# Output projection of a token-mixing stage: one full-precision product against three products of rounded parts, with GpSimd making one of the parts

## The reference

```
h = attention(x)                       # softmax(q k / 4) v, then the output projection w_out, b_out
h = concat([cls, h], tokens)
u = layernorm(h)
h = h + ssm(u)                         # Bu = u B_w.T; h_t = W h_{t-1} + Bu_t; y = hs C_w.T + D * u
u2 = layernorm(h)
shared = (silu(u2 Wg_s.T) * (u2 Wu_s.T)) Wd_s.T
p = sigmoid(u2 Wr.T + rb); the two best experts of 8 for each token
h = h + shared + sum over chosen e of p_e * expert_e(u2)
```

## Time and profile before

| | us |
|---|---|
| median of 3 runs | 1158.5 (1157.01 to 1158.73) |
| time of the profiled execution | 1163.81 |
| its span, first to last instruction | 1161.9 |
| around the span | 1.9 |
| PE busy | 1116.7 (96%) |
| DVE busy | 916.8 (79%) |
| ACT busy | 584.2 (50%) |
| POOL busy | 394.3 (34%) |
| mean granted TensorE clock | 0.987 |

### The profile page before, as it was taken

How to read it: one execution, slowest core, us unless ns; L and a number is a source line. 1 busy time by engine, 2 the same in 40 slices (tenths; PEclk the granted TensorE clock), 3 DMA queues, 4 the chain that set the end, 5 groups by cost and what they waited for, 6 DMA issues and landing times.

```text
span 1161.9 us, 22261 instructions
## 1 busy us (share of the span) xinstructions
PE 1116.7 (96%) x6090; PEld 718.5 (62%) x6091; DVE 916.8 (79%) x1571; ACT 584.2 (50%) x973; POOL 394.3 (34%) x508
## 2 busy tenths in 40 slices
PE   9999999999999999989999999969999999999996
PEld 5654333333333333477777787757888888888885
DVE  4788888888888887678888888777777777777774
ACT  4445777777777777631233222432444444444442
POOL 2002621011111101214345443353555555554553
PEclk9998999999999999989999999999999999999998
DMA  7887333332333322041244541122333333333332
GB/s 232 273 273 259 92 89 88 93 99 81 95 85 90 103 72 87 1 164 42 68 109 109 100 98 39 38 47 78 55 55 54 51 56 52 51 53 54 54 55 32
DMA packets 109714, 105.37 MB, mean 91 GB/s; under 512 B 42464, under 2 KB 97904, under 8 KB 109648
## 3 DMA queue, kind: packets, MB, share of 16 engines
q1 hardware_dynamic: 92704, 85.38, 26.2%
q0 software_dynamic: 16960, 19.38, 10.5%
HBM read 64.88 MB, written 39.68 MB: 90 GB/s over the span
## 4 chain that ended last, share of the span: by engine, by line
PE 73%; DVE 10%; issue 3%; POOL 3%; ACT 1%; another core or an unknown queue 0%; DMA 0%; POOLq 0%; DVEq 0%; ACTq 0%
PE mix_pairs L73 20%; PE pv L688 11%; PE by_key L675 10%; PE by_query L666 9%; PE mix_made L1874 9%; PE mix_turn L1861 3%; POOL kept_table L1130 3%; PE mix_made L1282 2%; PE mix_made L1270 2%; PE by_query L709 2%; PE mix_turn L1841 1%; PE mix_pairs L1308 1%; PE mix_made L1253 1%; DVE mix_stats L1462 1%; DVE k_mix_u L1472 1%
## 5 line engine op out<-in xcount | busy, mean ns | idle before, releaser
L762 DVE TENSOR_REDUCE k_neg_max<-by_query 128x2 f32<-128x1024 f32 x240 | 282.8, 1220 | 48.4 <-PE by_query L666 45.2
L823 ACT ACTIVATE k_wu_e<-by_key 128x512 f32<-128x512 f32 x512 | 270.1, 600 | 64.9 <-PE by_key L675 64.8
L675 PE MATMUL by_key<-k_wg_e 99*128 99x512 bf16 x512 | 175.1, 384 | 2.8 <-PEq L147 2.4
L1818 POOL DMA_INDIRECT out_rows<-x_y,k_slot x72 | 114.0, 1583 | 156.1 <-PE mix_turn L1841 104.6
L666 PE MATMUL by_query<-k_wg_e 96*128 96x512 bf16 x480 | 144.7, 382 | 0.0
L1918 ACT ACTIVATE x_gate<-mix_pairs 128x512 f32<-128x512 f32 x72 | 43.0, 597 | 196.8 <-PE mix_pairs L73 196.8
L688 PE MATMUL pv<-k_wu_e,k_wd_e 128*17 128x512 f32 x1024 | 134.5, 598 | 0.3 <-ACT k_wu_e L823 0.3
L73 PE MATMUL mix_pairs<-w_short,x_T 128*128 x288 | 120.8, 419 | 2.2 <-issue 2.2
L1874 PEld LDWEIGHTS mix_made<-x_wd,x_acts_T 128*128 128x128 f32 x864 | 111.2, 188 | 7.4 <-ACT x_acts_T L1941 0.9
L73 PE MATMUL mix_pairs<-w_short,x_rest 128*128 x288 | 113.9, 396 | 0.0
L1874 PE MATMUL mix_made<-x_wd,x_acts_T 128*128 128x256 f32 x864 | 112.6, 279 | 0.7 <-ACT x_acts_T L1941 0.7
(11 more groups left out here) (251 smaller groups left out, 1960.8 us busy)
## 6 DMA issues: line engine op xcount, KB each, us to landing
k_wg_e<-kept_qk SPq DMA_DIRECT2D x384, 64.0 KB, 2.3
kept_qk<-k_qk_parts SPq DMA_DIRECT2D x32, 384.0 KB, 3.4
kept_v<-k_v_ones SPq DMA_DIRECT2D x8, 544.0 KB, 5.3
k_wd_e<-kept_v SPq DMA_DIRECT2D x32, 136.0 KB, 2.7
k_wu_e<-in_xT SPq DMA_DIRECT2D x8, 512.0 KB, 4.6
kept_heads<-k_wd_e SPq DMA_DIRECT2D x8, 512.0 KB, 3.0
k_heads_in<-kept_heads SPq DMA_DIRECT2D x8, 512.0 KB
k_wg_e<-in_wg_e SPq DMA_DIRECT2D x8, 512.0 KB, 4.7
```

What stands on the lines that cost most here:

```text
L675: pe.matmul(by_key[:, key_bank(job), :], k_rows[0:SROWS, g, h, kt * P:(kt + 1) * P], q_rows[0:SROWS, g, h, :], start=True, stop=True).then ...
L762: dve.tensor_reduce(neg_max[:, g % 2, 2 * n:2 * n + 2], by_query[:, bank:bank + 2, :], AX.X, ALU.max, negate=True).then_inc(query_read, 1)
L823: act.activation(probs[:, key_tile(j) // 2 * G + j // 2 % G, j % 2, :], by_key[:, key_bank(job), :], ACT.Exp, scale=float(HD) ** -0.5).the ...
L1818: pool.indirect_dma_start(out=dram["out"], in_=y[:, r % 2, :], in_offset=None, compute_op=ALU.add, out_offset=bass.IndirectOffsetOnAxis(ap ...
```

## The change

The change has four parts.

1. For images 2 to 7, `project_out` takes three fp32r products (`split_products`) in the place of one float32 product per tile and chunk. It needs the rounded part and the rest of `heads_T` and of `wo_T`. ACT makes the rounded parts `heads_short` (128x1024, once for each of the images 2 to 7, in steps 1 to 6) and `wo_short` (128x512, once, in step 1), right behind its copy of `heads_T`. POOL makes the rests in place, right behind `+ h` and ahead of the power for the second layer norm: `mix_heads_T_rest` occupies the place of `heads_T`, `wo_T_rest` that of `wo_T`. Images 0 and 1 keep the float32 product.
2. `u2` is turned, rounded, cut and copied bank by bank: `u2_turned` is told after each of the two banks, and the three instructions on 128x1024 become three times two on 128x512 in steps 0 to 6. Step 7 keeps whole instructions.
3. The new tiles `heads_short` and `wo_short` lie where `wd_e` of experts 4 and 5 comes to lie, so these two matrices are loaded in step 7, behind the store of image 6's output, and no longer in steps 3 and 4.
4. Several semaphores of the class token are merged into one (`cls_products`), with the same waits in the same order.

The diff, cut to what does this:

```diff
@@ SP
-                for name in ("wg_e", "wu_e", "wd_e") if e < E - 2 else ("wg_e", "wu_e"):
+                for name in ("wg_e", "wu_e", "wd_e") if e < EARLY_DOWN else ("wg_e", "wu_e"):
...
                 if nxt:
                     load_expert(b + 1)
+                elif this:
+                    load_late("out_made", 2 * B, range(EARLY_DOWN, E - 2))
...
-                    load_late()
+                    load_late("gate_made", FC * B, (E - 2, E - 1))
@@ POOL, in step
                     pool.tensor_tensor(rows, rows, h[:, :, :], ALU.add).then_inc(ev["ud_done"], 1)
+                    if b == 1:
+                        pool.wait_ge(ev["heads_shortened"], 1)
+                        pool.wait_ge(ev["out_made"], 2 * (b + 1))
+                        pool.tensor_tensor(short(wo_parts[1][:, :, :]), mem["wo_T"][:, :, :], wo_parts[0][:, :, :],
+                                           ALU.subtract).then_inc(ev["heads_cut"], 1)
+                    if nxt and prev:
+                        pool.wait_ge(ev["heads_shortened"], b + 1)
+                        pool.tensor_tensor(short(heads_rest), heads_T, heads_parts[0][:, :, :],
+                                           ALU.subtract).then_inc(ev["heads_cut"], 1)
                     inverse_deviation(b, 2)
@@ ACT, in step
                 if nxt:
                     copy_turned(heads_T, b + 1, "heads_turned", "hT_copied")
+                if b == 1:
+                    act.activation(short(wo_parts[0][:, :, :]), mem["wo_T"][:, :, :],
+                                   ACT.Copy).then_inc(ev["heads_shortened"], 1)
+                if nxt and prev:
+                    act.wait_ge(ev["hT_copied"], b + 2)
+                    act.activation(short(heads_parts[0][:, :, :]), heads_T, ACT.Copy).then_inc(ev["heads_shortened"], 1)
                 if prev:
                     silu(b - 1, 3)
...
-                    copy_turned(short(u2_short), b, "u2_turned", "shared_shortened")
-
-                    act.wait_ge(ev["u2_cut"], b + 1)
-                    copy_turned(u2_T, b, "u2_turned", "u2T_copied")
+                    for c in range(DC):
+                        act.wait_ge(ev["u2_turned"], DC * b + c + 1)
+                        act.activation(short(u2_short[:, c, :]), turn[:, c, :], ACT.Copy).then_inc(ev["shared_shortened"], 1)
+
+                    for c in range(DC):
+                        act.wait_ge(ev["u2_cut"], DC * b + c + 1)
+                        act.activation(u2_T[:, c, :], turn[:, c, :], ACT.Copy).then_inc(ev["u2T_copied"], 1)
@@ PE
+                        if parts:
+                            mm = split_products(pe, to, [part[:, c, t * P:(t + 1) * P] for part in lhs],
+                                                [part[:, c, :] for part in w], start=(c == 0), stop=(c == DC - 1))
...
-                by_token(heads_T, mem["wo_T"], "out_made", tiles)
+                if b < 2:
+                    by_token(heads_T, mem["wo_T"], "out_made", tiles, False)
+                else:
+                    pe.wait_ge(ev["heads_cut"], b)
+                    by_token(heads_parts, wo_parts, "out_made", tiles, True)
@@ DVE, cut_second
+                    for c in range(DC):
+                        dve.wait_ge(ev["shared_shortened"], 2 + DC * b + c + 1)
+                        dve.tensor_tensor(short(u2_rest[:, c, :]), turn[:, c, :], u2_short[:, c, :],
+                                          ALU.subtract).then_inc(ev["u2_cut"], 1)
```

More of the change, by code:

```diff
@@ L903 @@
 EARLY = 5
+EARLY_DOWN = 4
 def shorten_weights(act, mem, n):
@@ L948, in stage_mix @@
             for n in ("mix_heads_T", "mix_u_T", "mix_hidden", "mix_u2_T", "u2_short", "u2_rest"))
+        heads_rest = mem["mix_heads_T_rest"][:, :, :].rearrange(by_feature, c=DC)
+        heads_parts, wo_parts = (mem["heads_short"], heads_rest), (mem["wo_short"], mem["wo_T_rest"])
         h2 = sb("mix_h2", [P, 2, TT, D], FP32)
@@ L1032, in load_expert, with load_late @@
             def load_expert(e):
-                for name in ("wg_e", "wu_e", "wd_e") if e < E - 2 else ("wg_e", "wu_e"):
+                for name in ("wg_e", "wu_e", "wd_e") if e < EARLY_DOWN else ("wg_e", "wu_e"):
                     sp.dma_start(mem[name][:, bass.ds(e, 1), :, :], dram[name][:, bass.ds(e, 1), :, :]
                                  ).then_inc(mem["expert_in"][e] if e < 3 else mem["experts_in"], 16)
-            def load_late():
-                sp.wait_ge(ev["gate_made"], FC * B)
-                for e in (E - 2, E - 1):
+            def load_late(free, count, which):
+                sp.wait_ge(ev[free], count)
+                for e in which:
                     sp.dma_start(mem["wd_e"][:, bass.ds(e, 1), :, :], dram["wd_e"][:, bass.ds(e, 1), :, :]
@@ L1203, in step @@
                 if last:
-                    copy_turned(u2_T, b, "u2_turned", "u2T_copied")
-                    act.wait_ge(ev["u2T_copied"], b + 1)
-                    act.activation(short(u2_short[:, :, :]), u2_T[:, :, :], ACT.Copy).then_inc(ev["shared_shortened"], 1)
+                    act.wait_ge(ev["u2_turned"], DC * (b + 1))
+                    act.activation(u2_T[:, :, :], turn[:, :, :], ACT.Copy).then_inc(ev["u2T_copied"], DC)
+                    act.wait_ge(ev["u2T_copied"], DC * (b + 1))
+                    act.activation(short(u2_short[:, :, :]), u2_T[:, :, :], ACT.Copy).then_inc(ev["shared_shortened"], DC)
                 elif this:
-                    copy_turned(short(u2_short), b, "u2_turned", "shared_shortened")
-                    act.wait_ge(ev["u2_cut"], b + 1)
-                    copy_turned(u2_T, b, "u2_turned", "u2T_copied")
+                    for c in range(DC):
[4 more added lines that the diff above has]
+                        act.activation(u2_T[:, c, :], turn[:, c, :], ACT.Copy).then_inc(ev["u2T_copied"], 1)
                 if this:
@@ L1233, in _, with turn_rows @@
         def _(pe):
-            def turn_rows(rows, done, to=turn):
+            def turn_rows(rows, done, to=turn, by_bank=False):
                 for c in range(DC):
@@ L1237, in turn_rows @@
                         mm = pe.transpose(to[:, c, t * P:(t + 1) * P], rows[:, t, c * P:(c + 1) * P], ident[:, :])
-                mm.then_inc(ev[done], 1)
+                    if by_bank:
+                        mm.then_inc(ev[done], 1)
+                if not by_bank:
+                    mm.then_inc(ev[done], 1)
             def turn_heads(b):
@@ L1476, in cut_second @@
             def cut_second(b):
-                dve.wait_ge(ev["shared_shortened"], 2 + b + 1)
-                dve.tensor_tensor(short(u2_rest[:, :, :]), turn[:, :, :] if b < B - 1 else u2_T[:, :, :], u2_short[:, :, :],
-                                  ALU.subtract).then_inc(ev["u2_cut"], 1)
+                if b == B - 1:
+                    dve.wait_ge(ev["shared_shortened"], 2 + DC * B)
+                    dve.tensor_tensor(short(u2_rest[:, :, :]), u2_T[:, :, :], u2_short[:, :, :],
+                                      ALU.subtract).then_inc(ev["u2_cut"], DC)
+                else:
+                    for c in range(DC):
+                        dve.wait_ge(ev["shared_shortened"], 2 + DC * b + c + 1)
+                        dve.tensor_tensor(short(u2_rest[:, c, :]), turn[:, c, :], u2_short[:, c, :],
+                                          ALU.subtract).then_inc(ev["u2_cut"], 1)
             def place(j, par):
@@ L1567, in step @@
                 if this:
-                    dve.wait_ge(ev["u2_turned"], b)
+                    dve.wait_ge(ev["u2_turned"], DC * b)
                     dve.wait_ge(ev["u2_stored"], 16 * b)
@@ L2146, in program @@
                         mem[part] = alias.enter_context(nc.sbuf_tensor(part, [P, TT, D], FP32))
+            if name in ("mix_heads_T", "wo_T"):
+                with ExitStack() as alias:
+                    mem[name + "_rest"] = alias.enter_context(nc.sbuf_tensor(name + "_rest", *kinds[name]))
             if name not in mem:
```

42 lines of the change are left out of this document (23 added, 19 removed).

## The result

The changed kernel takes 1176.42 us (median of 4 runs, 1175.73 to 1179.55), the kernel before 1158.62 beside it (4 runs, 1157.01 to 1159.04). The ratio is 1.016, with a 95% interval of 1.014 to 1.0181: slower by 17.8 us, where 1177.0 had been forecast.

A forecast was written before the change was run, and what follows sets the result against it. It took a middle mixing step to be bound by a loop through DVE and POOL that PE follows. 13.8 + 1.2 − 0.8 + 4.4 = 18.6 us on the median 1158.5 gave 1177, range 1166 to 1186.

The forecast's parts named there:

- The hold on DVE: Mixing recurrence: POOL's subtraction delays DVE 2.3 us in each of 6 steps, 13.8 us; `wo`'s rest adds 1.2 in step 1.
- The clock: PE before `make_y`: a 2.87 us pause lowers TensorE's clock in three of steps 2 to 6, 1.47 us each, 4.4 together.
- Bank by bank: Turn of `u2`: DVE's cut ends earlier in step 0, −0.8 us once; 0 in middle steps.
- PE's saving at 0: `project_out`: fp32r products save PE 0.50 us in each of 6 steps, off the loop, so 0 in time.
- The tie: Before the first norm's power: statistics needing `project_out` and the sixth scatter end together, 0.04 us apart, hiding PE's gain.
- ACT, the loads and the semaphores at 0: ACT's rounded parts fit its spare time; later loads of two down matrices and merged semaphores cost nothing: 0 us each.
- A: Rival: POOL holds DVE off as forecast but TensorE's clock does not fall, without the 4.4: 1172.7 us; chance 0.25.
- B: Rival: DVE's closely spaced sums keep POOL out until the recurrence is nearly over, nothing late: 1157.5 us; chance 0.13.
- C: Rival: PE bounds the steps after all, with no contention: 1154.7 us; chance 0.04.
- D: Rival: TensorE's clock falls in every step and stays low through `make_y`, up to 3.6 us each: 1194 us; chance 0.06.
- steps of 37.2 us or more: Sign expected in the changed kernel's trace: mixing steps with at least this period, where a middle step took 34.94 us.

The follow-up runs named there:

- run 1: The changed kernel, but POOL's subtraction waits for DVE's last sum of the recurrence (both hidden states out): 1157.74 us, ratio 0.9984 to the kernel before.
- run 5: The changed kernel with products nobody reads in PE's pause ahead of `make_y` (20 in step 1, 8 in each of steps 2 to 6): 1169.82 us.
- run 4: The changed kernel without its first part (float32 product in all steps, no rounded parts or rests): 1157.86 us, ratio 0.9987 to the kernel before.
- run 7: The kernel before, with only the power of the next image's first norm moved behind four scatters instead of six: 1158.78 us, ratio 0.9994.
- run 2: The changed kernel with POOL memsets, which write but read nothing, in place of its subtractions (rests are zero): 1157.45 us, ratio 0.9988 to the kernel before.
- run 6: The kernel of run 1, with the power of the next image's first norm behind four scatters instead of six: 1153.73 us, ratio 0.9954 to the kernel before.
- run 8: The changed kernel with all ACT and POOL work, but one float32 product, of the rests alone, for images 2 to 7: 1176.54 us.
- run 3: The changed kernel with each subtraction for the rest of the heads done twice, one behind the other: 1189.18 us, ratio 1.0258 to the kernel before.

## Why the prediction was right

The mechanism, its place, its size and the sign came out as forecast; the terms were right to some tenths, with misses that cancel in part. For the sum I compare the changed kernel with run 1, which does the same work with another place of the subtraction; from the power of step 0 to the second power of step 7 they take 257.24 and 237.96 us, 19.28 apart.

- **The hold on DVE**, the term of 13.8 for six steps and 1.2 for `wo`, 15.0 together: measured 5 × 2.02 + 2.93 = 13.0. I had POOL enter behind L1562 and DVE do the whole of its 0.69 behind POOL's end. In fact POOL entered a little before the recorded end of L1562 (its end 574.39 less 2.36 is 572.03, against 572.18), and L1563 ends 0.54 behind POOL (574.93). These two overlaps are the 0.3 a step that I had too much.
- **The clock**, the term of 4.4 for three falls: measured 3 × 1.42 = 4.3 in steps 2, 4 and 6. That three of five was right is luck: I had no row that decided it, and equal pauses of 2.60 and 2.59 went either way. Missed was step 1, for which I counted nothing, since before had its fall there already; behind the pause of 6.04 it costs more. Between the changed kernel (33.94 from the power of step 0 to the second of step 1) and run 5 (31.97), where nothing falls, lie 1.97 us, 0.5 more than the 1.47 of before's fall. Run 1 has no fall in step 1 (28.98, where before took 30.44 and run 4 took 30.30), so against it the whole 1.97 counts: 13.0 + 4.3 + 1.97 = 19.3, which closes the 19.28. Whether step 1 has its fall is chance as well: behind a pause of 3.14 us `make_y` took 3.92 in runs 1 and 7 and 5.41 in runs 2 and 6.
- **Bank by bank**: −0.8 forecast in step 0; measured −0.80 in run 4 and the changed kernel alike (8.79 for 9.59). In the middle steps I had said 0; it is −0.09 each.
- **PE's saving at 0**: right for the time (run 8, and 0.03 a step by run 1). The tie behind it I misread in two points. The power followed the statistics by 0.09, the same lag as in run 7, where nothing else can set it (588.12 to 588.21); so they set it, and not both. In run 1, where the sixth scatter sets it, the period is 0.12 shorter, and I had allowed 0.04. And the statistics weren't waiting for `project_out` but for the cut of `u2` (see run 6). The product's saving was 0.7 us and not 0.50 a step, since it takes 2.91 and not 3.12: the 0.13 each, read off a group of 12 with the last one's tail, was 0.12 in a longer row.
- **ACT, the loads and the semaphores at 0**: right (run 4).
- **The rivals.** A (the clock holds) is run 5 to a fair degree: 1169.82, 2.9 under its 1172.7; the smaller hold is 2.0, and the fall of before in step 1, which run 5 hasn't, 1.5. B (DVE keeps its turn) is refuted by L1563 and by run 3. C (PE bounds) is refuted by run 8. D (the clock falls in every step and stays low through `make_y`) occurred nowhere: steps 3 and 5 had no fall, and even in step 1 the clock came back inside `make_y`.

Against the kernel before the terms measure 13.0 + 4.3 + 0.5 − 0.8 − 0.7 = 16.3 us (the 0.5 is step 1's clock, the 0.7 six steps of 0.12), where I had added up 18.6. The mixing stage agrees: from the first power of step 0 to the last of step 7 it takes 249.70 us before and 266.03 after, 16.3 more. The medians lie 17.8 apart. No run shows where the other 1.5 us come from; from that last power to the end, the profiled executions of all kernels but before's take between 402.7 and 405.9 us, so they differ by more than that among themselves. That 1177.0 came within 0.6 us of 1176.4 is therefore luck in part: the hold was 2.0 too high, the middle steps 0.7, the clock 0.4 too low, and the rest is not in the terms at all. Of the signs I had named, "steps of 37.2 us or more" came in three middle steps of five; steps 3 and 5 had 36.84.

Two more points stay open. Why the clock falls behind one pause and not behind an equal one isn't shown by any run; neither is why before's profiled execution had the pause of 6.95 in step 8.

## What to carry to other kernels

Before work goes to an idle GpSimd, look at what VectorE does at that moment: if both read two operands from SBUF, most of the length of the GpSimd instruction (here 2.02 of 2.36 us) is laid on VectorE's chain, and TensorE's clock may add to it. The same instruction was free a few microseconds later, beside a VectorE instruction with an input in PSUM; so choose the place, with one wait if need be. And when a saving shows nothing because of a tie, look for the other side of the tie, and for what really sets each side: both edits together gave 0.46% where each alone gave at most 0.16%.

## What the runs showed of the hardware

- A GpSimd instruction that waits for the port got it even between two VectorE instructions that follow each other without a wait (run 3: 2.83 us for the second, where it takes 0.68). VectorE didn't keep the port by being busy.
- The scan is held off too (2.23 where it takes 1.26), and a GpSimd memset of 128x1024 (0.95 us) held off nothing (run 2).
- A GpSimd duration can include its own wait: 2.67 beside DVE, 2.36 alone, for the same instruction.
- Two pauses of TensorE equal to 0.01 us (2.60 and 2.59) had the granted clock at 0.50 behind the one and at 1.00 behind the other; a pause of 3.14 went both ways as well (`make_y` 5.41 in runs 2 and 6, 3.92 in runs 1 and 7). With products whose result nobody reads in the pause, `make_y` ran at full speed in all steps (3.92 or 3.93).
